# Attention and feed-forward in one kernel: the last batch's attention listed ahead of batch 14's gates, without idle matmuls

## The chip, the cores and the metric

One of the cores of a Trainium2 chip runs the kernel. The metric is the device time of one execution in microseconds (us). Of the kernel before, three timed runs and one profiled execution are shown. In the profile, PE is TensorE (PEld its weight loads), DVE is VectorE, ACT is ScalarE, POOL is GpSimd and SP is SyncE, which issues the transfers.

## The reference, cut to what matters

The input is x of 16 batches x 1024 rows x 256 columns in float32. `_layernorm` divides by sqrt(var + 1e-5) and has no weights.

```python
x = x + _layernorm(attn(_layernorm(x)))     # Q, K, V of width 256; softmax(Q K^T / 16) V
x = x + _layernorm(ffn(_layernorm(x)))      # h = silu(gate) * up, 768 wide; h @ w_down^T
```

Gate, up and down weights are integers times 1/127. Both residual additions take the unnormalised x.

## The kernel before

**Numbers and matmuls.** Every float32 operand of a large matmul is split into a high and a low half in float16 (`...h`, `...l`), and a product is made of two or three float16 passes, all recorded at line 868 (`passes`). One full line of work therefore is: an engine computes a float32 tile, ScalarE writes the high half (`o_high`, `y_high`, `p_high`, `h_high`), VectorE or GpSimd the low one (`o_low`, `y_low`, `p_low`, `h_low`), and where rows have to become columns SyncE turns both halves by a DMA transpose (`turn_x`, `turn_p`, `turn_y`).

**The work of one batch b.** The 1024 rows are 8 tiles of 128, in two groups g of four tiles. `project_z(b, g)` multiplies x by a product of the Q and K weights. `score(b, i)` makes the 128 x 1024 scores of tile i, 12 matmuls of 512 columns; `row_max`, `exp`, `p_high`, `p_low` and `turn_p` follow. `attend(b, g, u)` (line 1014) multiplies the turned probabilities by x, 12 matmuls of 512 columns; u // 2 is the half dh of the columns, u % 2 the first or second half of the keys. So four calls finish a group, and `o_high` (520) and `o_low` (751) of each dh follow its second call. `project_v(b, g)` (1028) applies the V weights, 24 matmuls of 256 columns, and leaves V of four tiles in the PSUM banks 4 and 5.

**From V to y.** VectorE scales V by the softmax sums (`y_scale`, 762, two tiles a call) and takes its statistics (`y_stats`, 771). GpSimd makes the inverse deviation (`y_norm`, 389: lines 327 and 331, then 334 and 336). VectorE adds to x and takes the statistics of the sum (`x1_add`, 783: line 790 twice, then 795 and 799; it reads the banks 4 and 5, half 0 bank 4, half 1 bank 5). GpSimd normalises again (`x1_norm`, 401). ScalarE writes y (`y_hat`, 526) and its high half (`y_high`, 534), GpSimd the low half (`y_low`, 409), SyncE turns both. Only then can `gate_up(b, g, c)` run (1042): 4 matmuls of 512 columns for the gate, 4 for up, in two neighbouring banks, for one of six chunks c of h.

**From gates to the result.** ScalarE applies `silu` (540), VectorE multiplies (`h_mul`, 801), then `h_high` (548) and `h_low` (415; VectorE makes it for c = 2 and 5, GpSimd for the others). The buffer `hf` has three places, so `silu` of chunk n waits for `h_low` of chunk n - 3. `down(b, g, pair)` (1051) multiplies by the down weights, 24 matmuls of 256 columns, into bank 4 (pair 0) or 5 (pair 1), the same banks as V. `d_stats`, `d_norm`, `d_add` and `add_bias` normalise and add, and `store` writes the result. The last group's down projection is `last_down`, followed by the functions `last_...`.

**What sets the order.** Every engine has a list of calls written out by hand, and runs it strictly in that order. An engine waits on semaphores inside a call; what is behind that call in its list waits too. A loop `for b in range(1, 13)` (PE; ScalarE's runs over 2 to 13) holds the steady state, in which batch b + 1's scores run among batch b's attention and gates. Behind the loop, batches 13 to 15 are listed call by call: from line 1184 for SyncE, 1341 for GpSimd, 1578 for ScalarE, 1886 for VectorE, 2107 for TensorE. The pair `(name, n)` in a TensorE call is what its bank waits for:

```python
            down(t, 14, 0, 0, (x1_done, 118), three)
            gate_up(t, 14, 1, 5, 2, (silu_done, 178), (hmul_done, 178), three)
            keep_busy(t, 36, ol_done[1], 32, 7)
            gate_up(t, 15, 0, 0, 6, (ol_done[0], 32), (ol_done[1], 32), three)
```

`(x1_done, 4n + k)` with n = 2b + g means that k tiles of group (b, g) have been added; `(ft_done[pair], 2n + 2)` that `d_add` has read the bank of that pair; `(silu_done, k)` and `(hmul_done, k)` that chunk k - 1, counted over all batches, has been read out of its bank. `keep_busy(t, n, sem, value, bank)` (892) issues n matmuls of 256 columns on a constant, whose result nobody reads; line 897 records them. There is one call of 36 of them, at line 2171, and two at the start of the program. `reload(s, b, g)` (260) loads x again for the residual sum into one of four buffers; its wait on `stored` is for the stores that last used that buffer. The calls of batch 14 and 15 that the text speaks of stand at the lines 2145 to 2188 (TensorE), 1716 to 1724 (the end of ScalarE's list), 1993 to 2005 (`x1_add` of batch 15), 1214 and 1240 (`reload`).

In the profiled run the flag is 0, so `three` is False: `gate_up` has 8 matmuls and `down` 24.

## Time and profile before

| what | before |
|---|---|
| median of three runs (lowest to highest) | 1363.91 us (1363.36 to 1363.94) |
| the profiled execution | 1363.66 us, of which the span of the profile 1361.90 us |
| TensorE busy | 1347.7 us, 99% of the span |
| VectorE, ScalarE, GpSimd busy | 901.8, 878.1, 832.4 us (66%, 64%, 61%) |
| granted clock of TensorE, mean | 1.00 |
| idle matmuls of line 897 | 66: 30 at the start, 36 behind line 2170 |
| HBM traffic | 39 GB/s over the span |

The span runs from the first to the last instruction of the trace. A row of a timeline gives the start and the duration in us, the engine, the line, the operation, its output and its inputs; xN means N such operations merged, and square brackets the idle time before them and what ended it. TensorE's matmuls overlap: each shows 0.38 us for 512 columns and 0.27 us for 256, but the next one starts before it ends, so the distance of two starts is what one costs.

### The profile page before, as it was taken

How to read it: one execution, taken by the hardware profiler on the slowest of the kernel's cores; microseconds unless marked ns; L12 is line 12 of the kernel's file. 1: busy time of each engine (PE TensorE's matmuls, PEld its weight loads, DVE VectorE, ACT ScalarE, POOL GpSimd, SP SyncE). 2: the span in 40 equal slices, each digit the busy share in tenths (PEclk: the TensorE clock that was granted, in tenths of full speed). 3: DMA queues.
4: the chain of work that ended last, by engine and by line, in shares of the span. 5: the costliest groups of instructions: out<-in, count | busy, mean ns of one | idle time of the engine just before them, and what ended most of it. 6: DMA issues, size and time to landing. Idle time of an engine off the chain costs nothing.

```text
span 1361.9 us, 22402 instructions
## 1 busy us (share of the span) xinstructions
PE 1347.7 (99%) x7414; PEld 725.8 (53%) x7414; DVE 901.8 (66%) x2167; ACT 878.1 (64%) x1378; POOL 832.4 (61%) x1001
## 2 busy tenths in 40 slices
PE   8999999999999999999999999999999999999998
PEld 5445455555555555555554555545555555555555
DVE  7895675666766666666766657667666676656556
ACT  6765775666757577475665766567566675756645
POOL 5686483765847648475584746748376584754635
PEclk9999999999999999999999999999999999999999
DMA  5996482835638366392753827448373563725512
GB/s 180 184 194 138 88 153 79 140 101 115 133 86 157 68 132 140 70 169 65 131 132 71 162 79 127 121 92 147 80 142 100 114 134 86 136 66 100 110 32 64
DMA packets 432968, 157.24 MB, mean 115 GB/s; under 512 B 413905, under 2 KB 416337, under 8 KB 432850
## 3 DMA queue, kind: packets, MB, share of 16 engines
q1 hardware_dynamic: 432048, 154.99, 55.2%
q8 instruction: 61, 1.00, 0.3%
q10 hardware_dynamic: 802, 0.79, 0.2%
q14 instruction: 57, 0.47, 0.1%
HBM read 36.70 MB, written 16.78 MB: 39 GB/s over the span
## 4 chain that ended last, share of the span: by engine, by line
PE 92%; POOL 2%; DVE 2%; DMA 2%; ACT 1%; issue 1%; SPq 0%; DVEq 0%; ACTq 0%; POOLq 0%
PE S L868 91%; DMA yTl<-yl 1%; POOL xl L368 1%; POOL Pl L386 0%; POOL yl L413 0%; DVE st L721 0%; DVE S L768 0%; DMA xs<-in_L_attn_t 0%; DVE mxs L739 0%; POOL xs L356 0%; PE S L897 0%; DVE st L777 0%; ACT yn L531 0%; DMA xTl<-xl 0%; POOL rs L331 0%
## 5 line engine op out<-in xcount | busy, mean ns | idle before, releaser
L511 ACT ACTIVATE P<-S,nmx,sc 128x1024 f32<-128x1024 f32 x128 | 153.6, 1200 | 267.1 <-DVE nmx L743 264.9
L805 DVE SCALAR_TENSOR_TENSOR hf<-S,sc,hf 128x512 f32<-128x512 f32 x192 | 141.9, 746 | 140.8 <-ACT hf L546 135.2
L739 DVE TENSOR_REDUCE mxs<-S 128x1 f32<-128x1024 f32 x128 | 156.1, 1220 | 115.7 <-PE S L868 115.7
L386 POOL TENSOR_TENSOR Pl<-P,Ph 128x1024 f16<-128x1024 f32 x96 | 205.1, 2138 | 30.1 <-issue 26.0
L868 PE MATMUL S<-PTh,xh 128*128 128x512 f16 x512 | 194.1, 379 | 0.0
L868 PE MATMUL S<-PTl,xh 128*128 128x512 f16 x512 | 194.0, 379 | 0.0
L868 PE MATMUL S<-PTh,xl 128*128 128x512 f16 x512 | 194.0, 379 | 0.0
L868 PE MATMUL S<-xTh,zTh 128*128 128x512 f16 x506 | 191.8, 379 | 2.0 <-ACT P L511 1.0
L868 PE MATMUL S<-xTh,zTl 128*128 128x512 f16 x508 | 192.5, 379 | 0.0
L868 PE MATMUL S<-xTl,zTh 128*128 128x512 f16 x508 | 192.5, 379 | 0.0
L327 POOL TENSOR_SCALAR rs<-mv,sc 128x2 f32<-128x2 f32 (+2 forms) x96 | 34.6, 361 | 227.4 <-DVE mv L781 184.9
L422 POOL TENSOR_TENSOR hTl<-hf,hTh 128x512 f16<-128x512 f32 x128 | 146.4, 1158 | 42.4 <-ACT hTh L553 42.4
L868 PE MATMUL S<-Wh,hTh 128*128 128x256 f16 x768 | 170.3, 273 | 0.0
L868 PE MATMUL S<-Wh,hTl 128*128 128x256 f16 x768 | 170.3, 273 | 0.0
L546 ACT ACTIVATE hf<-S,sc 128x512 f32<-128x512 f32 x192 | 130.6, 682 | 52.5 <-POOL hTl L422 37.7
L331 POOL TENSOR_TENSOR rs<-rs,mhalf 128x4 f32<-128x4 f32 (+2 forms) x160 | 145.5, 909 | 13.3
L868 PE MATMUL S<-yTh,Gh 128*128 128x512 f16 x384 | 145.6, 379 | 2.4 <-DMA yTl<-yl 2.4
L868 PE MATMUL S<-yTl,Gh 128*128 128x512 f16 x384 | 145.5, 379 | 0.0
L868 PE MATMUL S<-yTh,Uh 128*128 128x512 f16 x384 | 145.5, 379 | 0.0
L868 PE MATMUL S<-yTl,Uh 128*128 128x512 f16 x384 | 145.5, 379 | 0.0
L553 ACT ACTIVATE hTh<-hf 128x512 f16<-128x512 f32 x192 | 119.5, 624 | 35.4 <-DVE hf L805 35.4
L518 ACT ACTIVATE Ph<-P 128x1024 f16<-128x1024 f32 x128 | 134.8, 1054 | 4.2 <-DMA PTl<-Pl 1.1
(155 smaller groups left out, 2486.0 us busy)
## 6 DMA issues: line engine op xcount, KB each, us to landing
xs<-in_L_attn_t SPq DMA_DIRECT2D x32, 512.0 KB, 5.3
...
out_x<-X SPq DMA_DIRECT2D x62, 256.0 KB, 2.9
PTh<-Ph SPq DMA_TRANSPOSE x128, 3.2
PTl<-Pl SPq DMA_TRANSPOSE x128, 3.2
...
```

The costliest lines, as they stand in the source:

```text
L327: p.engine.tensor_scalar(rs, var, scalar1=eps, scalar2=mul, op0=ALU.add, **({} if mul is None else {"op1": ALU.mult})).then_inc(g_step, 1)
L331: return p.engine.tensor_tensor(out=rs, in0=rs, in1=mhalf[:, 0:rs.shape[1]], op=ALU.pow)
L368: p.engine.tensor_tensor(out=xl[k][:, gs, :], in0=src, in1=xh[k][:, gs, :], op=ALU.subtract).then_inc(xl_done if b else xl0_done, 1)
L386: p.engine.tensor_tensor(out=Pl[:, m % 3, :], in0=P[:, m % 2, :], in1=Ph[:, m % 3, :], op=ALU.subtract).then_inc(pl_vector if i in PL_ON_V ...
L422: p.engine.tensor_tensor(out=hTl[g][:, c, :], in0=hf[:, n % 3, :], in1=hTh[g][:, c, :], op=ALU.subtract).then_inc(hl_vector if c in HL_ON_ ...
L511: a.engine.activation(P[:, m % 2, :], ps[:, bank:bank + 2, :].rearrange("p a n -> p (a n)"), ACT.Exp, bias=nmx[:, c:c + 1], scale=sS, accu ...
L518: a.engine.activation(Ph[:, m % 3, :], P[:, m % 2, :], ACT.Copy).then_inc(ph_done, 1)
L546: a.engine.activation(hf[:, n % 3, :], ps[:, bank, :], ACT.Silu, scale=sc2[:, 3:4]).then_inc(silu_done, 1)
L553: a.engine.activation(hTh[g][:, c, :], hf[:, n % 3, :], ACT.Copy).then_inc(hh_done, 1)
L739: v.engine.tensor_reduce(mxs[:, c:c + 1], ps[:, bank:bank + 2, :].rearrange("p a n -> p (a n)"), axis=AX.X, op=ALU.max, negate=True).then_ ...
L805: v.engine.scalar_tensor_tensor(out=hf[:, n % 3, :], in0=ps[:, bank + 1, :], scalar=sc2[:, 4:5], in1=hf[:, n % 3, :], op0=ALU.mult, op1=AL ...
L868: done = t.engine.matmul(out, s, m, start=(start and i == 0), stop=(stop and i == len(terms) - 1))
```

## The change

The lists of all five engines behind the loop are written anew; no function changes. In TensorE's list `attend(15, 0, 3)` and `project_v(15, 0)` go ahead, all of batch 15's attention and both of its V projections stand in front of the last three gates of batch 14, `down(14, 0, 0)` and `down(14, 0, 1)` go behind those, and the 36 idle matmuls are gone. The pairs that the four `down` calls and the `project_v` calls wait for follow the new order of use of the banks 4 and 5. In the other lists calls change places; the number of calls of each kind is the same. `last_bias` moves from the end of ScalarE's list to the middle of batch 15's gates. The diff, cut to its core:

```diff
--- before.py
+++ after.py
@@ -1183,68 +1183,68 @@
+            store(s, 12, 0, 0)
             turn_p(s, 14, 0, 0)
             turn_p(s, 14, 0, 1)
-            store(s, 12, 0, 0)
             store(s, 12, 0, 1)
+            reload(s, 14, 0)
             turn_p(s, 14, 1, 0)
+            turn_p(s, 14, 2, 0)
             turn_p(s, 14, 1, 1)
-            turn_p(s, 14, 2, 0)
             turn_p(s, 14, 2, 1)
             turn_p(s, 14, 3, 0)
...
+            turn_x(s, 15, 0, 0)
             turn_y(s, 13, 0, 1)
-            turn_x(s, 15, 0, 0)
             turn_x(s, 15, 0, 1)
+            turn_x(s, 15, 1, 0)
             turn_p(s, 14, 5, 0)
+            turn_x(s, 15, 1, 1)
             turn_p(s, 14, 5, 1)
             turn_p(s, 14, 6, 0)
             turn_p(s, 14, 6, 1)
-            turn_x(s, 15, 1, 0)
-            turn_x(s, 15, 1, 1)
             turn_p(s, 14, 7, 0)
-            turn_p(s, 14, 7, 1)
             turn_y(s, 13, 1, 0)
             turn_y(s, 13, 1, 1)
             store(s, 12, 1, 0)
             store(s, 12, 1, 1)
-            reload(s, 14, 0)
+            turn_p(s, 14, 7, 1)
...
+            reload(s, 15, 0)
             turn_p(s, 15, 5, 1)
             turn_p(s, 15, 6, 0)
             turn_p(s, 15, 6, 1)
-            store(s, 13, 0, 1)
             turn_y(s, 14, 1, 0)
             turn_y(s, 14, 1, 1)
             turn_p(s, 15, 7, 0)
+            store(s, 13, 1, 1)
             turn_p(s, 15, 7, 1)
-            store(s, 13, 1, 1)
-            reload(s, 15, 0)
             reload(s, 15, 1)
-            store(s, 14, 0, 0)
-            store(s, 14, 0, 1)
             turn_y(s, 15, 0, 0)
             turn_y(s, 15, 0, 1)
             turn_y(s, 15, 1, 0)
             turn_y(s, 15, 1, 1)
+            store(s, 14, 0, 0)
+            store(s, 14, 0, 1)
...
@@ -1338,26 +1338,26 @@
             x_low(p, 15, 0)
             p_low(p, 14, 5)
+            x_low(p, 15, 1)
+            p_low(p, 14, 6)
             y_norm(p, 13, 1)
-            p_low(p, 14, 6)
-            x_low(p, 15, 1)
-            p_low(p, 14, 7)
+            h_low(p, 13, 0, 0)
             x1_norm(p, 13, 1)
-            h_low(p, 13, 0, 0)
+            z_low(p, 15, 0)
             d_norm(p, 12, 1, 0)
             y_low(p, 13, 1)
             h_low(p, 13, 0, 1)
-            z_low(p, 15, 0)
+            h_low(p, 13, 0, 3)
             d_norm(p, 12, 1, 1)
-            h_low(p, 13, 0, 3)
             h_low(p, 13, 0, 4)
+            p_low(p, 14, 7)
...
@@ -1366,34 +1366,34 @@
+            p_low(p, 15, 7)
             h_low(p, 14, 0, 4)
-            p_low(p, 15, 7)
             h_low(p, 14, 1, 0)
-            d_norm(p, 14, 0, 0)
+            y_norm(p, 15, 0)
             h_low(p, 14, 1, 1)
-            d_norm(p, 14, 0, 1)
-            y_norm(p, 15, 0)
-            h_low(p, 14, 1, 3)
             x1_norm(p, 15, 0)
             y_low(p, 15, 0)
             y_norm(p, 15, 1)
+            h_low(p, 14, 1, 3)
             h_low(p, 14, 1, 4)
             x1_norm(p, 15, 1)
+            d_norm(p, 14, 0, 0)
+            d_norm(p, 14, 0, 1)
             y_low(p, 15, 1)
...
@@ -1575,133 +1575,134 @@
+            exp(a, 14, 2, 0)
             p_high(a, 14, 1)
-            exp(a, 14, 2, 0)
             p_high(a, 14, 2)
             exp(a, 14, 3, 2)
+            o_high(a, 13, 1, 1)
             p_high(a, 14, 3)
-            o_high(a, 13, 1, 1)
             exp(a, 14, 4, 0)
             p_high(a, 14, 4)
...
+            o_high(a, 15, 0, 1)
             silu(a, 14, 0, 5, 2)
+            silu(a, 14, 1, 0, 0)
             h_high(a, 14, 0, 5)
-            silu(a, 14, 1, 0, 0)
-            add_bias(a, 13, 1, 1)
+            h_high(a, 14, 1, 0)
             silu(a, 14, 1, 1, 2)
-            h_high(a, 14, 1, 0)
             h_high(a, 14, 1, 1)
+            o_high(a, 15, 1, 0)
+            y_hat(a, 15, 0, 0)
+            o_high(a, 15, 1, 1)
             silu(a, 14, 1, 2, 0)
-            h_high(a, 14, 1, 2)
-            o_high(a, 15, 0, 1)
-            add_bias(a, 14, 0, 0)
-            silu(a, 14, 1, 3, 2)
-            add_bias(a, 14, 0, 1)
-            h_high(a, 14, 1, 3)
-            o_high(a, 15, 1, 0)
-            o_high(a, 15, 1, 1)
-            silu(a, 14, 1, 4, 0)
-            y_hat(a, 15, 0, 0)
             y_hat(a, 15, 0, 1)
             y_high(a, 15, 0)
+            h_high(a, 14, 1, 2)
+            silu(a, 14, 1, 3, 2)
+            silu(a, 14, 1, 4, 0)
+            h_high(a, 14, 1, 3)
             h_high(a, 14, 1, 4)
             silu(a, 14, 1, 5, 2)
+            y_hat(a, 15, 1, 0)
+            silu(a, 15, 0, 0, 6)
+            y_hat(a, 15, 1, 1)
+            silu(a, 15, 0, 1, 0)
             h_high(a, 14, 1, 5)
-            silu(a, 15, 0, 0, 6)
-            y_hat(a, 15, 1, 0)
-            y_hat(a, 15, 1, 1)
             y_high(a, 15, 1)
-            silu(a, 15, 0, 1, 0)
+            silu(a, 15, 0, 2, 2)
             h_high(a, 15, 0, 0)
-            silu(a, 15, 0, 2, 2)
             h_high(a, 15, 0, 1)
             h_high(a, 15, 0, 2)
+            add_bias(a, 14, 0, 0)
+            add_bias(a, 14, 0, 1)
             silu(a, 15, 0, 3, 6)
+            last_bias(a)
             silu(a, 15, 0, 4, 0)
+            silu(a, 15, 0, 5, 2)
             h_high(a, 15, 0, 3)
-            silu(a, 15, 0, 5, 2)
             h_high(a, 15, 0, 4)
...
@@ -1720,7 +1721,6 @@
             add_bias(a, 15, 0, 1)
-            last_bias(a)
             last_centre(a)
@@ -1902,131 +1902,131 @@
...
             z_float(v, 15, 0, 0)
             h_mul(v, 13, 0, 1, 2)
             d_stats(v, 12, 1, 0)
             h_mul(v, 13, 0, 2, 6)
+            d_add(v, 12, 1, 0)
             d_stats(v, 12, 1, 1)
-            h_low(v, 13, 0, 2)
             h_mul(v, 13, 0, 3, 0)
             h_mul(v, 13, 0, 4, 2)
-            d_add(v, 12, 1, 0)
             z_float(v, 15, 1, 6)
+            d_add(v, 12, 1, 1)
+            h_low(v, 13, 0, 2)
             h_mul(v, 13, 0, 5, 0)
-            d_add(v, 12, 1, 1)
             h_mul(v, 13, 1, 0, 2)
+            h_mul(v, 13, 1, 1, 6)
             h_low(v, 13, 0, 5)
-            h_mul(v, 13, 1, 1, 6)
...
             h_mul(v, 14, 0, 0, 6)
+            h_mul(v, 14, 0, 1, 0)
             x1_add(v, 14, 1, 0)
-            h_mul(v, 14, 0, 1, 0)
             h_mul(v, 14, 0, 2, 2)
+            h_mul(v, 14, 0, 3, 6)
             x1_add(v, 14, 1, 1)
-            h_mul(v, 14, 0, 3, 6)
-            h_low(v, 14, 0, 2)
             row_max(v, 15, 7, 2)
             h_mul(v, 14, 0, 4, 0)
+            h_low(v, 14, 0, 2)
             d_stats(v, 13, 1, 1)
             row_inverse(v, 15, 1)
             d_add(v, 13, 1, 1)
+            o_low(v, 15, 0, 0)
+            o_low(v, 15, 0, 1)
             h_mul(v, 14, 0, 5, 2)
-            o_low(v, 15, 0, 0)
+            h_mul(v, 14, 1, 0, 0)
             h_low(v, 14, 0, 5)
-            h_mul(v, 14, 1, 0, 0)
+            y_scale(v, 15, 0, 0)
+            y_stats(v, 15, 0, 0)
+            y_scale(v, 15, 0, 1)
+            y_stats(v, 15, 0, 1)
             h_mul(v, 14, 1, 1, 2)
-            d_stats(v, 14, 0, 0)
-            d_stats(v, 14, 0, 1)
-            h_mul(v, 14, 1, 2, 0)
-            d_add(v, 14, 0, 0)
-            h_low(v, 14, 1, 2)
-            d_add(v, 14, 0, 1)
-            o_low(v, 15, 0, 1)
-            y_scale(v, 15, 0, 0)
-            y_scale(v, 15, 0, 1)
-            y_stats(v, 15, 0, 0)
-            y_stats(v, 15, 0, 1)
-            h_mul(v, 14, 1, 3, 2)
             x1_add(v, 15, 0, 0)
             x1_add(v, 15, 0, 1)
             o_low(v, 15, 1, 0)
             o_low(v, 15, 1, 1)
+            h_mul(v, 14, 1, 2, 0)
+            y_scale(v, 15, 1, 0)
+            y_stats(v, 15, 1, 0)
+            y_scale(v, 15, 1, 1)
+            y_stats(v, 15, 1, 1)
+            h_mul(v, 14, 1, 3, 2)
             h_mul(v, 14, 1, 4, 0)
-            y_scale(v, 15, 1, 0)
-            y_scale(v, 15, 1, 1)
-            y_stats(v, 15, 1, 0)
-            y_stats(v, 15, 1, 1)
+            x1_add(v, 15, 1, 0)
+            x1_add(v, 15, 1, 1)
+            h_low(v, 14, 1, 2)
+            d_stats(v, 14, 0, 0)
             h_mul(v, 14, 1, 5, 2)
-            x1_add(v, 15, 1, 0)
+            d_stats(v, 14, 0, 1)
+            d_add(v, 14, 0, 0)
+            h_mul(v, 15, 0, 0, 6)
+            d_add(v, 14, 0, 1)
+            h_mul(v, 15, 0, 1, 0)
             h_low(v, 14, 1, 5)
-            x1_add(v, 15, 1, 1)
-            h_mul(v, 15, 0, 0, 6)
-            h_mul(v, 15, 0, 1, 0)
             h_mul(v, 15, 0, 2, 2)
             d_stats(v, 14, 1, 0)
...
@@ -2152,31 +2152,30 @@
             down(t, 13, 1, 1, (x1_done, 120), three)
             attend(t, 15, 0, 0, (silu_done, 172))
             attend(t, 15, 0, 1)
+            attend(t, 15, 0, 3)
             gate_up(t, 14, 0, 5, 2, (exp_done, 128), (exp_done, 128), three)
             gate_up(t, 14, 1, 0, 0, (silu_done, 173), (hmul_done, 173), three)
+            project_v(t, 15, 0, (ft_done[0], 56), (ft_done[1], 56))
+            attend(t, 15, 1, 0, (ol_done[0], 31))
             gate_up(t, 14, 1, 1, 2, (silu_done, 174), (hmul_done, 174), three)
-            down(t, 14, 0, 0, (x1_done, 118), three)
-            down(t, 14, 0, 1, (ft_done[1], 56), three)
-            gate_up(t, 14, 1, 2, 0, (silu_done, 175), (hmul_done, 175), three)
-            attend(t, 15, 0, 3)
-            attend(t, 15, 1, 0, (ol_done[0], 31))
-            project_v(t, 15, 0, (ft_done[0], 58), (ft_done[1], 58))
-            gate_up(t, 14, 1, 3, 2, (silu_done, 176), (hmul_done, 176), three)
             attend(t, 15, 1, 1)
             attend(t, 15, 1, 2, (ol_done[1], 31))
             attend(t, 15, 1, 3)
+            gate_up(t, 14, 1, 2, 0, (silu_done, 175), (hmul_done, 175), three)
+            project_v(t, 15, 1, (x1_done, 122), (x1_done, 124))
+            gate_up(t, 14, 1, 3, 2, (silu_done, 176), (hmul_done, 176), three)
             gate_up(t, 14, 1, 4, 0, (silu_done, 177), (hmul_done, 177), three)
-            project_v(t, 15, 1, (x1_done, 122), (x1_done, 124))
             gate_up(t, 14, 1, 5, 2, (silu_done, 178), (hmul_done, 178), three)
-            keep_busy(t, 36, ol_done[1], 32, 7)
+            down(t, 14, 0, 0, (x1_done, 126), three)
+            down(t, 14, 0, 1, (x1_done, 128), three)
             gate_up(t, 15, 0, 0, 6, (ol_done[0], 32), (ol_done[1], 32), three)
             gate_up(t, 15, 0, 1, 0, (silu_done, 179), (hmul_done, 179), three)
             gate_up(t, 15, 0, 2, 2, (silu_done, 180), (hmul_done, 180), three)
-            down(t, 14, 1, 0, (x1_done, 126), three)
+            down(t, 14, 1, 0, (ft_done[0], 58), three)
             gate_up(t, 15, 0, 3, 6, (silu_done, 181), (hmul_done, 181), three)
             gate_up(t, 15, 0, 4, 0, (silu_done, 182), (hmul_done, 182), three)
             gate_up(t, 15, 0, 5, 2, (silu_done, 183), (hmul_done, 183), three)
-            down(t, 14, 1, 1, (x1_done, 128), three)
+            down(t, 14, 1, 1, (ft_done[1], 58), three)
             gate_up(t, 15, 1, 0, 6, (silu_done, 184), (hmul_done, 184), three)
             gate_up(t, 15, 1, 1, 0, (silu_done, 185), (hmul_done, 185), three)
             down(t, 15, 0, 0, (ft_done[0], 60), three)
```

## Rows read from the trace of the kernel before

**Rows 1.** The page: busy time, the chain that ended last, DMA issues

```profile
PE 1347.7 (99%) x7414; PEld 725.8 (53%) x7414; DVE 901.8 (66%) x2167; ACT 878.1 (64%) x1378; POOL 832.4 (61%) x1001
...
PE 92%; POOL 2%; DVE 2%; DMA 2%; ACT 1%; issue 1%; SPq 0%; DVEq 0%; ACTq 0%; POOLq 0%
...
out_x<-X SPq DMA_DIRECT2D x62, 256.0 KB, 2.9
```

**Rows 2.** Waits of TensorE from 40 us on: total us, times, longest us

```profile
PE S L868 <- DMA yTl<-yl: 2.4, 4, 1.4
PE S L868 <- ACT P L511: 1.0, 1, 1.0
```

**Rows 3.** Stretches: length, busy time of PE, PEld, DVE, ACT, POOL, granted clock, DMA

```profile
101.00:104.00 3.00, 2.56 (x12) 1.18 (x13) 0.76 (x2) 2.97 (x5) 1.13 (x3) 1.00 1.03 197
1300.00:1320.00 20.00, 20.00 (x123) 11.77 (x122) 14.67 (x45) 8.74 (x15) 9.10 (x15) 1.00 0.18 41
...
1360.00:1362.00 2.00, 0.00 (x0) 0.00 (x0) 0.00 (x0) 0.00 (x0) 0.00 (x0) 0.74 0.33 122
```

**Rows 4.** Timeline of TensorE

```profile
1195.80 0.38 PE L868 MATMUL S<-yTh,Gh 128*128 128x512 f16 x1
...
1266.39 0.39 PE L868 MATMUL S<-xTh,zTh 128*128 128x512 f16 x1
...
1313.54 0.27 PE L868 MATMUL S<-Vh,oTl 128*128 128x256 f16 x1
1313.65 0.38 PE L868 MATMUL S<-yTh,Gh 128*128 128x512 f16 x1
...
1315.38 0.82 PE L897 MATMUL S<-ident 128*128 128x256 f16 x6
...
1319.42 0.39 PE L868 MATMUL S<-yTh,Gh 128*128 128x512 f16 x1
```

**Rows 5.** Timeline of SyncE's DMA queue

```profile
1144.17 1.06 SPq L288 DMA_DIRECT2D out_x<-X  x2
...
1191.87 1.23 SPq L282 DMA_TRANSPOSE yTl<-yl  x1
...
1316.30 1.23 SPq L282 DMA_TRANSPOSE yTl<-yl  x1
```

**Rows 6.** Transfers into yTl between 1300 and 1340 us

```profile
DMA to landing us min/median/max: 3.1/3.1/3.1
```

**Rows 7.** Timeline of VectorE

```profile
1264.94 1.39 DVE L805 SCALAR_TENSOR_TENSOR hf<-S,sc,hf 128x512 f32<-128x512 f32 x2
...
1299.96 1.67 DVE L768 SCALAR_TENSOR_TENSOR S<-S,rinv,bvb 128x256 f32<-128x256 f32 x4 [3.89 <-PE S L868]
...
1313.85 1.67 DVE L768 SCALAR_TENSOR_TENSOR S<-S,rinv,bvb 128x256 f32<-128x256 f32 x4 [1.92 <-PE S L868]
...
1318.83 0.88 DVE L790 SCALAR_TENSOR_TENSOR X<-S,rs,X 128x256 f32<-128x256 f32 x2 [0.92 <-POOL rs L331]
...
1321.09 0.87 DVE L790 SCALAR_TENSOR_TENSOR X<-S,rs,X 128x256 f32<-128x256 f32 x2
...
1356.08 0.43 DVE L837 BATCH_NORM_STATS2 st<-S 128x6 f32<-128x256 f32 x1 [0.46 <-PE S L868]
...
1357.16 1.66 DVE L861 SCALAR_TENSOR_TENSOR X<-zw,rs,X 128x256 f32<-128x256 f32 x4
```

**Rows 8.** Timeline of GpSimd

```profile
1310.10 0.23 POOL L336 TENSOR_SCALAR nb<-nb 128x4 f32<-128x4 f32 x1
...
1317.76 1.04 POOL L331 TENSOR_TENSOR rs<-rs,mhalf 128x4 f32<-128x4 f32 x1
```

**Rows 9.** Timeline of ScalarE

```profile
1309.46 0.60 ACT L524 ACTIVATE oTh<-S 128x512 f16<-128x512 f32 x1 [4.29 <-PE S L868]
...
1310.91 2.06 ACT L531 ACTIVATE yn<-X,nb,rs 128x256 f32<-128x256 f32 x4
...
1354.35 1.69 ACT L571 ACTIVATE X<-X,c 128x256 f32<-128x256 f32 x4
```

More of the change, by code:

```diff
@@ L1226, in _ @@
             turn_y(s, 14, 0, 0)
+            turn_p(s, 15, 4, 0)
             turn_y(s, 14, 0, 1)
-            turn_p(s, 15, 4, 0)
+            store(s, 13, 0, 1)
             turn_p(s, 15, 4, 1)
             turn_p(s, 15, 5, 0)
+            reload(s, 15, 0)
             turn_p(s, 15, 5, 1)
@@ L1340, in _ @@
                 x_norm(p, b + 3, 1)
+            p_low(p, 14, 2)
             y_norm(p, 13, 0)
-            p_low(p, 14, 2)
+            p_low(p, 14, 3)
             x1_norm(p, 13, 0)
-            p_low(p, 14, 3)
             y_low(p, 13, 0)
@@ L1368, in _ @@
             p_low(p, 15, 0)
+            p_low(p, 15, 2)
             y_norm(p, 14, 0)
-            p_low(p, 15, 2)
             x1_norm(p, 14, 0)
@@ L1404, in _ @@
             h_low(p, 15, 1, 0)
+            h_low(p, 15, 1, 1)
             d_norm(p, 15, 0, 0)
-            h_low(p, 15, 1, 1)
             h_low(p, 15, 1, 3)
@@ L1587, in _ @@
             y_hat(a, 13, 0, 1)
+            o_high(a, 13, 1, 0)
             y_high(a, 13, 0)
-            o_high(a, 13, 1, 0)
             x_high(a, 15, 0)
+            x_high(a, 15, 1)
             exp(a, 14, 5, 2)
             p_high(a, 14, 5)
-            x_high(a, 15, 1)
             exp(a, 14, 6, 0)
@@ L1621, in _ @@
             silu(a, 13, 1, 3, 2)
-            add_bias(a, 12, 1, 1)
             h_high(a, 13, 1, 2)
@@ L1628, in _ @@
             h_high(a, 13, 1, 5)
+            add_bias(a, 13, 0, 0)
             o_high(a, 14, 0, 1)
             o_high(a, 14, 0, 0)
-            add_bias(a, 13, 0, 0)
+            add_bias(a, 13, 1, 0)
             exp(a, 15, 0, 0)
+            exp(a, 15, 1, 2)
             p_high(a, 15, 0)
-            exp(a, 15, 1, 2)
             p_high(a, 15, 1)
@@ L1637, in _ @@
             p_high(a, 15, 2)
-            add_bias(a, 13, 1, 0)
             exp(a, 15, 3, 2)
+            o_high(a, 14, 1, 0)
             p_high(a, 15, 3)
-            o_high(a, 14, 1, 0)
             y_hat(a, 14, 0, 0)
+            y_hat(a, 14, 0, 1)
             exp(a, 15, 4, 0)
-            p_high(a, 15, 4)
-            y_hat(a, 14, 0, 1)
             y_high(a, 14, 0)
             o_high(a, 14, 1, 1)
+            p_high(a, 15, 4)
+            add_bias(a, 13, 0, 1)
             exp(a, 15, 5, 2)
@@ L1932, in _ @@
             h_mul(v, 13, 1, 5, 0)
+            h_low(v, 13, 1, 5)
             d_stats(v, 13, 0, 0)
-            h_low(v, 13, 1, 5)
             d_add(v, 13, 0, 0)
+            o_low(v, 14, 0, 1)
             d_stats(v, 13, 1, 0)
-            o_low(v, 14, 0, 1)
+            d_add(v, 13, 1, 0)
             o_low(v, 14, 0, 0)
@@ L2011, in _ @@
             h_mul(v, 15, 0, 3, 6)
+            d_add(v, 14, 1, 0)
             h_mul(v, 15, 0, 4, 0)
-            d_add(v, 14, 1, 0)
             h_mul(v, 15, 0, 5, 2)
+            h_low(v, 15, 0, 5)
             d_stats(v, 14, 1, 1)
-            h_low(v, 15, 0, 5)
+            h_mul(v, 15, 1, 0, 6)
             d_add(v, 14, 1, 1)
-            h_mul(v, 15, 1, 0, 6)
             h_mul(v, 15, 1, 1, 0)
```

68 lines of the change are left out of this document (34 added, 34 removed).

## The prediction

> **What bounds the kernel.** I read the page first: TensorE is busy 99% of the span and carries 92% of the chain that ended last, while VectorE, ScalarE and GpSimd are at 61 to 66% [rows 1]. So a change counts only where TensorE waits, where it does work that need not be done, and in what follows its last matmul. The waits of TensorE come next: from 40 us on it stands still for 3.4 us in all, its longest waits being 1.4 and 1.0 us [rows 2], and the same view from 1130 us on, where the edits lie, has no line for it. In the table of stretches the 20 us from 1300 hold 20.00 us of TensorE work at a granted clock of 1.00 [rows 3]. Dense, but not all useful: 36 of those matmuls are `keep_busy` (line 2171), from 1315.38 to the first matmul of `gate_up(15,0,0)` at 1319.42 [rows 4]. That is 4.04 us, in which the kernel in truth waits for batch 15's first y: its low half is issued for turning at 1316.30 and lands 3.1 us later, at 1319.4 [rows 5, 6]. The matmul starts at that moment, so the fillers just cover the wait.
>
> **Units.** The eight matmuls of 512 columns of one `gate_up` take 1.73 us (1313.65 to 1315.38), so two start 0.216 us apart; two of 256 columns start 0.11 us apart [rows 4], 0.109 over a long run. So `attend` and `score` (12 of 512) take 2.59 us, `gate_up` (8 of 512) 1.73 us, `project_v` and `down` (24 of 256) 2.62 us. The diff leaves the number of real matmuls as it is; only their order changes.
>
> **TensorE's order.** I put the calls end to end with these units. Both kernels run `attend(15,0,1)` up to about 1279.8 (in the time of before). Then, after: `attend(15,0,3)`, two gates, `project_v(15,0)` from 1285.9 to 1288.5, where before it is 1297.1 to 1299.8: batch 15's attention is 11.3 us ahead. Between the end of `project_v(15,0)` and `gate_up(15,0,0)` before has 15.6 us of work and the fillers; after has four attends, five gates, one `project_v` and two downs: 2.59 x 4 + 1.73 x 5 + 2.62 x 3 = 26.9 us. The chain from V to y took 19.4 us (1299.96, the first scaling, to 1319.4) [rows 5 to 7], so it is covered with some 7 us to spare, and **the 4.04 us go**.
>
> **What the new order puts in the way.** `down(14,0,0)` writes the bank from which `x1_add(15,1,0)` still reads V, and now waits for `(x1_done, 126)`. Before, with 1313.65 as the next call's first matmul after `project_v(15,1)`, the scaling starts at 1313.85 and the pair of adds runs 1318.83 to 1319.71 [rows 4, 7]: 6.06 us. Inside lie 3.4 us of scaling and statistics and the inverse deviation on GpSimd, which ends at 1318.80 [rows 8]. In the new list `h_mul(14,1,3)` and `h_mul(14,1,4)`, 0.73 us each, fall into GpSimd's 1.5 us and cost nothing; scaling and statistics are only interleaved. TensorE starts 0.06 us after such a product (1264.94 + 1.39 = 1266.33, to 1266.39) [rows 4, 7], so at 6.12. Up to there it has three gates, 5.19 us. **A new wait of 0.93 us.** Behind it in TensorE's queue stand both downs and all of batch 15's gates, so all of it counts. `down(14,0,1)` wants the second pair of adds, 2.3 us later than the first by their rows [rows 7], less some 0.6 for the `h_low` between them that is now behind: 1.7, under the 2.62 us of the first down. Bounds of the wait: 0.4 us if the adds come half a microsecond sooner, 1.6 if an `h_mul` misses its gap (0.73).
>
> The second half of `gate_up(14,1,5)` wants `h_mul(14,1,3)`, ready some 0.2 us too late; that shifts nothing, as `down` waits longer anyway. Further on, `silu(14,1,5)` waits behind the adds and `h_low(14,1,2)`; its product is ready about 11.5 us after `project_v(15,1)`, `gate_up(15,0,2)` wants it at 14.8. `down(14,1,0)` wants `h_low(14,1,5)` in its second half at 17.2; I work it out at 16.2.
>
> **The feed of the moved calls.** `project_v(15,0)` needs `o_high(15,0,1)` and `o_low(15,0,1)` after `attend(15,0,3)`: 0.6 us [rows 9] and 0.7 (like an `h_mul` on the same engine, half of 1.39 [rows 7]) under two gates, 3.45 us. `project_v(15,1)` has one gate (1.73 us) over the same pair, as before; but ScalarE now has `y_hat(15,0,0)` ahead of `o_high(15,1,1)`. Its input came 10.4 us after the scaling began (1299.96 to 1310.33) [rows 7, 8], so at 1299.1 where the scaling starts at 1288.7; two of its tiles take 1.04 [rows 9], to 1300.2; `attend(15,1,3)` ends at 1300.75. Spare: 0.55 us, cost nothing. If the cover goes, each further microsecond costs one.
>
> **Batches 13 and 14 in the new lists.** TensorE's order is unchanged there and dense. One wait vanishes: the second half of `score(15,7)` was due at 1266.32 and stood 0.07 us for `h_mul(14,0,2)` [rows 4, 7]; that product ends 0.7 us earlier once `h_mul(14,0,1)` is listed ahead of `x1_add(14,1,0)`. The narrowest places: turning y of (13,1) was issued at 1191.87, `gate_up(13,1,0)` begins at 1195.80 [rows 4, 5]; with 3.1 us to land, 0.8 us are spare. GpSimd now has `z_low(15,0)` (2.7 us) ahead of `y_low(13,1)` and `p_low(14,7)` (2.1 us) behind it; going through its list I get the issue 0.2 us later, up to 0.6. And `h_low(13,0,2)` now stands behind `d_add(12,1,1)`, so `silu(13,0,5)` comes some 2 us later, at about 1198.2, and its product by 1199.4; the second half of `gate_up(13,1,2)`, 4.3 us after 1195.80, wants it at 1200.1. Cost nothing, bound 0.5 us each.
>
> **SP's queue.** `reload(14,0)` now waits for the landing of both stores of (12,0) with `turn_p(14,1,0)` to the last behind it: issued until about 1145.2 [rows 5], landing 2.9 us later [rows 1], plus up to 2 us of issue, till 1150. `turn_p(14,1,0)` gets its input only at about 1151.1, as `exp(14,2)` now goes first; no loss. `reload(15,0)` holds `turn_p(15,5,1)`, for which `attend(15,1,0)` asks some 28 us later. The stores of (14,0) go behind the turnings of (15,y), since their downs are now late; ahead of them they would have closed the queue.
>
> **The end.** `last_bias` leaves ScalarE's end: 1.69 us from 1354.35 [rows 9], which the chain of waits counts as critical. But VectorE takes the statistics of the last tile at 1356.08, as soon as TensorE is done, and its four last adds follow without a gap, 1.66 us from 1357.16 [rows 7]. So 0, bound 0.1 us of gain. At its new place it holds `silu(15,0,4)` until about 1328.0; its bank is wanted at 1333.6.
>
> **Sum:** -4.04 + 0.93 - 0.07 = **-3.2 us**. The profiled execution took 1363.66 us for a span of 1361.90; it stands 0.25 below the median of the runs, 1363.91. So some 1360.7 as median. About 0.2% (2.7 us, a limit at 1361.2) is what a measurement of this kernel tells from no change; the forecast is 0.5 us past it.
>
> **The clock.** The granted clock stayed at 1.00 through the wait of 1.4 us at 101 us [rows 2, 3]; it fell (0.74 over the last 2 us) only when TensorE had done nothing since about 1356 [rows 3, 7]. So the new wait costs its own length. The Trainium skill, "TensorE: Matmul & The Clock Gate" (section "Part 1: The HAM clock gate"), says that half rate is the default and recent activity lifts it; by that rule idle products are worth their time where a wait would be long, which speaks against taking them out. Here the rows leave the sum at -3.2.
>
> **Rivals.**
> (A) The forecast, one new wait of 0.4 to 1.6 us: 1360.2 to 1361.4. Chance 0.57.
> (B) No new wait, as the adds come early enough: -4.1, 1359.8. Against it: the adds' 6.06 us hold a fixed order of work on two engines. 0.08.
> (C) A second wait upstream, 1 to 2.5 us: ScalarE's `y_hat(15,0,0)` holds `o_high(15,1,1)` and so `project_v(15,1)`, or y of (13,1) or `silu(13,0,5)` comes late. For it: spares of 0.5 to 0.9 us, worked out from many rows, in a schedule never seen. 1361.7 to 1363.3, say 1362.4. 0.23.
> (D) Nothing gained: the edited lists of VectorE, ScalarE and GpSimd lose in batches 13 and 14 what the fillers give, 3 to 4 us. 1363.9. 0.07.
> (E) Slower: at the wait before `down(14,0,0)` the clock falls to the lower of its two levels. Price: a gate is 1.73 us dearer, a down 2.62. It decides from 3.2 us of such loss, two downs (5.2 us), which gives 1365.9. Against it: the clock rows above. 0.05.
> By the Trainium skill's rule, were it to bite, the time is that of (E).
>
> **Numbers.** Faster: A nearly whole (0.52), B (0.08), a little of C (0.05): 0.65. Same: the rest of A, most of C, D: 0.29. Slower: 0.06. The range begins just under (B), at 1359.7, and takes in most of C, to 1362.9; above it stay D, E and the end of C, some 0.15, below it next to nothing.
>
> **What would show it.** Right: no L897 row after 100 us; TensorE's waits list DVE X L790, once, 0.4 to 1.6 us, near 1310; turning of (15,0) issued near 1304.5 and 1306.6; last adds near 1354; clock 1.00. Wrong: waits on ACT oTh or DVE oTl (C), on DMA yTl or DVE hf between 1130 and 1280 (C, D), a clock below 1.00 after 1310 (E), or no wait at all (B).

## The result, and the profile after

The changed kernel takes **1361.71 us** (median of 22 runs, 1361.10 to 1362.43) against 1364.19 for the kernel before (22 runs, 1363.09 to 1364.78) on the same chip. The ratio is 0.9983, 95% interval 0.9977 to 0.9989: 2.48 us less, a little under the 0.2% (2.7 us) that the prediction took as the line to no change, though the interval leaves out 1. The forecast was 3.2 us less. Its profiled execution took 1361.76 us for a span of 1359.9. A few executions of the later runs took 200 to 3000 us longer at a lower granted clock, and every measured time given for a kernel is the median of the others.

The page, against [rows 1]: TensorE is 3.1 us less busy, with 36 matmuls fewer, and still carries by far the largest share of the chain that ended last, now 88% where it was 92%.

```profile
PE 1344.6 (99%) x7378; PEld 722.2 (53%) x7378; DVE 903.6 (66%) x2167; ACT 877.1 (65%) x1378; POOL 831.5 (61%) x1001
...
PE 88%; DVE 3%; POOL 2%; DMA 2%; SPq 2%; issue 1%; ACT 1%; DVEq 0%; ACTq 0%; POOLq 0%
```

Waits of TensorE from 40 us on (total us, times, longest), against [rows 2]: the last line is new, and it is the only wait behind 1130 us.

```profile
PE S L868 <- DMA yTl<-yl: 2.5, 4, 1.6
PE S L868 <- ACT P L511: 1.0, 1, 1.0
PE S L868 <- DVE X L790: 0.9, 1, 0.9
```

Timeline of TensorE, against [rows 4]: the first matmul of `down(14,0,0)` with its wait, and the last matmul of all. The one ahead of the wait starts at 1310.24 and the next was due at 1310.46, so it costs 1.01 us.

```profile
1311.47 0.27 PE L868 MATMUL S<-Wh,hTh 128*128 128x256 f16 x1 [0.85 <-DVE X L790]
...
1353.03 0.27 PE L868 MATMUL S<-Wh,hTl 128*128 128x256 f16 x1
```

Timeline of VectorE, against [rows 7]: the pair of `h_mul` in the gap that GpSimd leaves, the pair of adds that TensorE waits for (it ends at 1311.32), and the last adds, 2.7 us earlier than before.

```profile
1308.79 1.39 DVE L805 SCALAR_TENSOR_TENSOR hf<-S,sc,hf 128x512 f32<-128x512 f32 x2
1310.44 0.88 DVE L790 SCALAR_TENSOR_TENSOR X<-S,rs,X 128x256 f32<-128x256 f32 x2 [0.26 <-POOL rs L331]
...
1354.43 1.67 DVE L861 SCALAR_TENSOR_TENSOR X<-zw,rs,X 128x256 f32<-128x256 f32 x4
```

SyncE's queue, against [rows 5]: the turnings of batch 15's first y, `store(15,0,1)`, and the two last stores, of which the second waits for the last add.

```profile
1304.71 1.24 SPq L282 DMA_TRANSPOSE yTh<-yh  x1
1306.92 1.23 SPq L282 DMA_TRANSPOSE yTl<-yl  x1
...
1350.34 0.33 SPq L288 DMA_DIRECT2D out_x<-X  x1
1355.72 1.98 SPq L295 DMA_DIRECT2D out_x<-X  x2
```

The two last stores of the kernel before:

```profile
1358.45 1.05 SPq L295 DMA_DIRECT2D out_x<-X  x2
```

**Where the rest went.** Behind the last add the span runs on for 1359.9 - 1356.10 = 3.8 us; before it was 1361.9 - 1358.82 = 3.1. So 0.7 us were lost behind the last computation, and the last matmul and the last add kept their distance (3.05 and 3.07 us). The spans of these two traces lie only 2.0 us apart, since in the trace of the changed kernel what is ahead of `project_v(14,1)`, where TensorE's order is unchanged, took 0.40 us longer (it starts at 1255.89 us against 1255.49); over all 14 traces that start lies between 1254.65 and 1256.74. Two views of the transfers show where, each from 1.3 us ahead of the end of the last add: GB/s in 40 slices of a stretch of 4.5 us, what the queue q8 moved (the view calls it an instruction queue), and issue to landing. First before:

```profile
GB/s 0 0 0 0 146 0 0 0 0 0 0 0 0 0 0 137 300 382 382 410 437 355 437 410 301 264 355 346 146 0 0 0 0 0 0 0 0 0 0 0
...
q8 instruction: 1, 0.02, 1.6%
...
out_x<-X SPq DMA_DIRECT2D x1, 128.0 KB, 2.5
```

Then after:

```profile
GB/s 0 0 0 0 0 0 0 0 0 0 0 0 146 0 0 191 328 355 300 410 382 382 410 410 137 0 27 27 27 27 173 309 373 264 82 18 27 0 0 0
...
q8 instruction: 1, 0.02, 1.5%
...
out_x<-X SPq DMA_DIRECT2D x1, 128.0 KB, 3.3
```

The lone 146 is a transfer of 16 KB on q8, from here on the fetch. In most of the run one comes for some 128 matmuls (after: 129, 125 and 129 start between those at 1215.6, 1238.3, 1260.2 and 1285.4 us), so it is probably TensorE that is fed. The last ones come closer: between the three at 1348.2, 1353.2 and 1356.2 lie 44 matmuls and none, and no run shows what sets them. The fetch keeps one of the 16 DMA engines for 1.15 us (1.6% of 16 x 4.5). Before, it starts 0.84 us ahead of the end of the last add and is over at +0.31; the stores' data begin at about +0.4 and flow in one piece. After, it starts 0.12 us behind that end and is over at +1.20, so it overlaps the stores' data. Right behind it, from +1.5 on, the stores fall to 27 GB/s for half a microsecond. That is one packet of 3 KB in each slice, about a fifteenth of the full rate, as if only the engine that had the fetch were still at work on its share. SyncE's issue of the last store takes 1.58 us, where before it took 0.66, and the data flow again 0.45 us after it ends. Both last stores land in 3.3 us, where before they took 2.7 and 2.5.

The Trainium skill's page "DMA: Bandwidth & Descriptors" (section "Queues, rings and completion order") says that a DMA engine takes its queues in turn and changes only at the end of a packet. The rows fit that, but do not prove it: the view counts the fetch as one packet, and the store's share of one engine comes late behind it. Which engine it is they do not show.

### The profile page after: what moved, and what is told of

It reads as the page before. It is cut to its first block, busy times and chain, and to the rows that moved or that the text cites. A ratio compares the mean times of both kernels' runs of the same rounds, so it can differ in the third digit from the quotient of the medians.

```text
span 1359.9 us, 22330 instructions
## 1 busy us (share of the span) xinstructions
PE 1344.6 (99%) x7378; PEld 722.2 (53%) x7378; DVE 903.6 (66%) x2167; ACT 877.1 (65%) x1378; POOL 831.5 (61%) x1001
## 4 chain that ended last, share of the span: by engine, by line
PE 88%; DVE 3%; POOL 2%; DMA 2%; SPq 2%; issue 1%; ACT 1%; DVEq 0%; ACTq 0%; POOLq 0%
PE S L868 88%; DMA yTl<-yl 1%; SPq L276 1%; DVE S L768 1%; POOL xl L368 1%; DVE st L777 1%; POOL Pl L386 1%; DVE mxs L739 0%; POOL yl L413 0%; SPq L257 0%; DVE st L721 0%; ACT Ph L518 0%; POOL rs L331 0%; POOL xs L356 0%; DMA xs<-in_L_attn_t 0%
```

## The experiments

Two measures are used beside the time. **TensorE's part** is the time from a call whose order is the same in both kernels to the last matmul: from the first matmul of `project_v(14,1)`, 100.28 us before and 97.14 after; from that of `project_v(15,0)`, 66.87 after (the other traces with after's order agree to 0.01 from that second call on). **Early** and **late** tell where `d_add(15,0,1)` stands on VectorE: ahead of `h_mul(15,1,5)`, as in after, or behind `h_low(15,1,5)`, as before. **The tail** is from the end of the last add to the end of the span. Ratios are to the kernel before, run on the same chip.

### The changed kernel again

Edit: none.

> The changed kernel unaltered, for a second trace on the chip that the next kernels share. Three accounts of why the measured gain is 2.5 us where the sum gave 3.2. Theory 1 (the last stores): the two last transfers to out_x are always issued and landed later when store (15, 0, 1) has gone out some 5 us ahead of them; then the span again ends 3.7 to 3.9 us after the end of the last addition, against 3.1 in the trace of before, and the gain is 2.4 to 2.6 us. Rival 2 (chance): the issue of these stores varies from execution to execution by some 0.7 us; then this trace may as well show 3.1 us. Rival 3 (drift): before and after differed by up to 0.4 us in stretches where their code is the same, against the changed kernel; then a second trace may have the loop's end 0.3 to 0.4 us earlier. The wait of TensorE for the addition of y to x at the head of down (14, 0, 0) stands again, 0.8 to 1.1 us, in every account.

Measured: 1361.77 us, ratio 0.9984 (0.9975 to 0.9993). TensorE's part is 97.14 again, the wait at `down(14,0,0)` too, the tail 3.9 us. The 0.7 us behind the last add are lost again, which speaks against chance, and against drift as an account of the tail. The start of `project_v(14,1)` did move, to 1255.30 us, so drift there is real, and the measured 2.07 us under before is a little less than the first 2.48.

### What of the end does it

`end_back` is the changed kernel with this edit, `end_back2` the same once more, and `end_alone` is the kernel before with the reverse edit.

```diff
-            d_add(v, 15, 0, 1)
             h_mul(v, 15, 1, 5, 2)
             h_low(v, 15, 1, 5)
+            d_add(v, 15, 0, 1)
```

> The changed kernel with one thing put back: d_add (15, 0, 1) behind h_mul and h_low (15, 1, 5) on VectorE, as before the change, so that store (15, 0, 1) is issued some 4 us later, right ahead of the last stores. Theory 1 (the last stores lose 0.7 us where that store has gone out early): the span ends 3.0 to 3.2 us after the last addition and the kernel takes 0.5 to 0.7 us less than the changed one. Rival 2 (chance): equal to the changed kernel within 0.2 us in the median. Nothing of TensorE waits for h_mul (15, 1, 5) in the trace of the changed kernel, so TensorE's stretch stays the same in either account.

Measured: 1360.86 us, ratio 0.9978 (0.9968 to 0.9987), 0.91 us under the changed kernel on the same chip. TensorE's part stays at 97.14, the tail is 3.5 us. Theory 1 had the direction right and the size of the tail (3.0 to 3.2) too small; of the 0.9 us the traces show only 0.4 in the tail (3.9 to 3.5).

> The kernel before with one part of the change alone: d_add (15, 0, 1) ahead of h_mul (15, 1, 5) on VectorE. TensorE's work is untouched. Theory 1: the span ends 3.7 to 3.9 us after the last addition instead of 3.1, and the kernel takes 0.5 to 0.7 us more than before. Rival 2: the same as before within 0.2 us. If h_mul (15, 1, 5) were late for down (15, 1, 0) by the 0.6 us of the addition, TensorE would show a wait of up to 0.6 us there; the trace of the changed kernel shows none.

Measured: 1364.81 us, ratio 1.0009 (1.0000 to 1.0018), 0.97 us over before. TensorE's part 100.27, the tail 4.0 us. Both ways round, the early place of one call of 0.87 us on VectorE, which hides in idle time, costs 0.9 to 1.0 us of the whole.

`store_late` is the changed kernel with

```diff
+            s.wait_ge(last_st, 3)
             store(s, 15, 0, 1)
```

> The changed kernel with store (15, 0, 1) held back on SP until the statistics of the last tiles are there (near 1352.5 us instead of 1350.3), and nothing moved on VectorE. It parts the two things that end_back did together. Seen so far: with that store 5.4 us ahead of the first last store the span ended 3.8 to 4.0 us after the last addition (three traces), with 4.0 us between them 3.1 to 3.5 us (three traces). Theory 1 (the distance of the stores decides): with 3 us between them the span ends 3.0 to 3.4 us after the last addition and the time is 0.5 to 1.0 us below the changed kernel's. Rival (the order on VectorE decides, or it is chance): as the changed kernel within 0.2 us, 3.8 to 4.0 us after the last addition.

Measured: 1361.77 us, ratio 0.9978 (0.9969 to 0.9987), tail 3.7 us. The store is now 3.0 us ahead of the last ones, nearer than the 4.0 of before, and yet the tail is longer than before's 3.1. So in this trace the distance of the stores, theory 1 as put there, does not set the tail. The time speaks less plainly: the ratio is that of `end_back`, and 2.74 us under before on its chip is 0.3 to 0.7 more than the changed kernel (measured twice) and `after_shift` reached, while the profiled execution, 1362.49 us, is one of the slowest of its eleven. So one trace speaks against theory 1, and the time leaves it open. What orders the tails is when the 16 KB fetch is over; the table below has them all.

### The fillers

`no_fill` is the kernel before with

```diff
-            keep_busy(t, 36, ol_done[1], 32, 7)
```

> The kernel before without its 36 matmuls that compute nothing (the keep_busy call ahead of gate_up (15, 0, 0)); nothing else is changed. TensorE then waits for o_low (15, 1, 1) and the yTl of batch 15 instead of filling the time. Theory (these matmuls only cover a wait, the order sets the time): a wait of 3.9 to 4.1 us stands in their place, the granted clock stays at 1.00 behind it, and the time is that of before within 0.3 us. Rival (clock): a stretch of 4 us without matmuls brings TensorE to the lower clock for the gates of batch 15 behind it; at 2.6 us for half a gate set, several us more, so over 1 us slower than before. Rival (the matmuls held something up): faster by 0.1 us or more.

Measured: 1365.88 us, ratio 1.0016 (1.0008 to 1.0025): 2.0 us **slower**. The theory fell on the clock and the time, its wait of 3.9 us is there, and the rival with the clock holds. TensorE's part is 102.83, 2.55 us more than before. Stretches of this kernel (columns as in [rows 3]):

```profile
1315.00:1316.00 1.00, 0.00 (x0) 0.00 (x0) 1.00 (x6) 0.00 (x0) 0.43 (x1) 1.00 0.78 145
1316.00:1317.00 1.00, 0.00 (x0) 0.00 (x0) 1.00 (x4) 0.00 (x0) 0.39 (x2) 0.98 0.36 73
1317.00:1318.00 1.00, 0.00 (x0) 0.00 (x0) 0.08 (x2) 0.63 (x1) 0.95 (x1) 0.50 1.01 189
...
1322.00:1323.00 1.00, 1.00 (x4) 0.43 (x3) 0.75 (x1) 0.00 (x0) 0.83 (x2) 0.50 0.00 0
1323.00:1324.00 1.00, 1.00 (x5) 0.34 (x3) 0.00 (x0) 0.00 (x0) 0.82 (x3) 0.61 0.00 0
```

And its timeline of TensorE:

```profile
1318.59 0.61 PE L868 MATMUL S<-yTh,Gh 128*128 128x512 f16 x1 [3.89 <-DMA yTl<-yl]
1318.99 0.63 PE L868 MATMUL S<-yTl,Gh 128*128 128x512 f16 x1
...
1323.69 0.43 PE L868 MATMUL S<-yTh,Uh 128*128 128x512 f16 x1
1323.95 0.38 PE L868 MATMUL S<-yTl,Uh 128*128 128x512 f16 x1
```

TensorE has nothing to do from 1314.7 on; near 1317 the granted clock goes to 0.50, the level of 1.2 GHz, and stays there until 1323.7. Twelve matmuls in a row take 5.10 us (1318.59 to 1323.69) where 12 x 0.216 = 2.6 would do: the 2.5 us lost. It was back at 1.00 behind them. So the idle products of before did not only cover a wait, they kept the clock. The Trainium skill's rule, given in the prediction from "TensorE: Matmul & The Clock Gate" (section "Part 1: The HAM clock gate"), is borne out here. The changed kernel can do without them because its order has no such wait: its own is 1.0 us, through which the clock stays at 1.00.

`fill_back` is the changed kernel with

```diff
+            keep_busy(t, 36, ol_done[1], 32, 7)
             gate_up(t, 15, 0, 0, 6, (ol_done[0], 32), (ol_done[1], 32), three)
```

> The changed kernel with the 36 matmuls that compute nothing put back in front of gate_up (15, 0, 0). Theory (in the new order nothing is left there to wait for, so they are pure time): TensorE's work ends 3.9 to 4.1 us later than in the changed kernel and the time is 3.8 to 4.2 us above it, near 1365.7 us. Rival (the changed order only moved the wait, and part of the 4 us would be spent waiting in any case): less than 3 us above it, and other waits of TensorE behind the call go.

Measured: 1366.30 us, ratio 1.0013 (1.0004 to 1.0022), 0.0030 above the changed kernel's 0.9983, or 4.1 us. From `project_v(15,0)` to the last matmul it is 70.80 us against 66.87, 3.93 more. In the new order nothing is waited for there.

### The new wait

`gate_only` is the changed kernel with

```diff
+            gate_up(t, 15, 0, 0, 6, (ol_done[0], 32), (ol_done[1], 32), three)
             down(t, 14, 0, 0, (x1_done, 126), three)
             down(t, 14, 0, 1, (x1_done, 128), three)
-            gate_up(t, 15, 0, 0, 6, (ol_done[0], 32), (ol_done[1], 32), three)
```

> The changed kernel with gate_up (15, 0, 0) ahead of down (14, 0, 0) on TensorE, nothing else moved. The wait of 1.0 us for the addition goes, since the gate covers 1.73 us of it and its own inputs landed at 1310.0, 0.4 us before it is due. Worked out from the trace of the changed kernel, the time comes back as a wait at down (14, 1, 0) or at a gate of batch 15, as h_low (14, 1, 5) and h_high (14, 1, 5) are queued behind silu and h_mul of batch 15: theory A: a new wait of 0.7 to 1.0 us there, within 0.3 us of the changed kernel. Rival B (those steps move up with TensorE): 0.9 to 1.1 us less than the changed kernel, no wait of TensorE over 0.2 us behind 1303 us.

Measured: 1364.47 us, ratio 0.9999 (0.9990 to 1.0008), where the changed kernel has 0.9983; from `project_v(15,0)` to the last matmul it is 68.91 us, 2.04 more. Neither theory has that. TensorE's waits behind 1303 us:

```profile
PE S L868 <- DVE hTl L422: 1.8, 1, 1.8
PE S L868 <- DMA yTl<-yl: 0.9, 1, 0.9
```

The first was foreseen in kind and was mis-sized by a factor of two. The second was not foreseen. The granted clock stayed at 1.00 through both.

`gate_first` is `gate_only` with both calls moved up, on ScalarE and on VectorE:

```diff
             y_hat(a, 15, 1, 0)
+            h_high(a, 14, 1, 5)
...
-            h_high(a, 14, 1, 5)
...
             d_stats(v, 14, 0, 1)
+            h_low(v, 14, 1, 5)
...
-            h_low(v, 14, 1, 5)
```

> The kernel gate_only with h_high (14, 1, 5) right behind y_hat (15, 1, 0) on ScalarE and h_low (14, 1, 5) right behind d_stats (14, 0, 1) on VectorE, so that what down (14, 1, 0) needs is done sooner. Theory: no wait of TensorE is left behind 1303 us and the kernel takes 0.9 to 1.1 us less than the changed one, near 1360.8 us. Rival: the added work ahead of silu (15, 0, 0) and h_mul (15, 0, 0) makes the gates of batch 15 late, and 0.3 us or less is gained.

Measured: 1362.03 us, ratio 0.9983 (0.9974 to 0.9992), no gain over the changed kernel. The wait for `hTl` is gone and that for `yTl` stays: from `project_v(15,0)` to the last matmul 66.96. The turning into `yTl` was issued in time, at 1307.07, but landed after 4.6 us. GB/s in 40 slices from 1308 to 1312 us:

```profile
GB/s 0 0 210 174 215 212 197 202 166 54 18 0 0 0 0 0 3 8 8 10 10 8 10 10 10 102 276 297 287 277 22 0 0 0 0 0 0 0 0 0
...
q8 instruction: 1, 0.02, 2.2%
...
yTl<-yl SPq DMA_TRANSPOSE x1, 4.6
```

The fetch began at 1308.25. The turning stops near 1309.1, trickles at 10 GB/s, and catches up from 1310.4 on. In `gate_only` the fetch began at 1309.50 and the landing took 4.5 us.

`gf_shift` is `gate_first`, and `after_shift` the changed kernel, with this edit of `keep_busy`, whose calls at the start are left:

```diff
-            for _ in range(n):
-                t.engine.matmul(ps[:, bank, 0:256], words[:, 0:128], words[:, :], start=True, stop=True)
+            for _ in range(2 * n):
+                t.engine.matmul(ps[:, bank, 0:128], words[:, 0:128], words[:, 0:128], start=True, stop=True)
```

> The kernel gate_first with each matmul of 256 columns in the two calls of keep_busy at the start (24 and 6 of them, behind 3 us and 12 us) replaced by two of 128 columns: the same columns, and 30 more matmuls with their weight loads in TensorE's stream of instructions, 1300 us ahead of the place in question. In gate_first and gate_only a 16 KB transfer of the queue that fetches instructions (q8, one for every 128 or so matmuls) started at 1308.25 and 1309.50, among the packets of the transpose into yTl, whose landing took 4.6 and 4.5 us instead of 3.1, and TensorE waited 0.9 us for it. Theory (this collision ate the gain): the fetch now falls some 4 to 5 us earlier, ahead of both transposes or on the first of them, yTl lands in 3.1 to 3.3 us, the wait of 0.9 us goes or shrinks under 0.3, and the kernel takes 0.6 to 1.0 us less than gate_first, if the fetch at the end stays where it is. Rival (the landing is long for another reason, as the order of TensorE's work): 4.5 us again and no difference from gate_first beyond 0.2 us.

Measured: 1360.37 us, ratio 0.9975 (0.9965 to 0.9985), against 0.9983 for `gate_first`; the two intervals overlap, so here the traces carry the argument. The fetch is at 1302.72, `yTl` lands in 3.1 us, TensorE has no wait behind 1303, and its part from `project_v(15,0)` is 65.87: 1.09 less than `gate_first`, 1.00 less than after. The same turning, GB/s from 1307 to 1311 us:

```profile
GB/s 0 0 0 97 220 215 223 220 207 220 205 197 220 192 190 165 51 0 0 0 0 0 0 0 0 0 0 0 0 0 0 0 0 0 0 0 0 0 0 0
...
yTl<-yl SPq DMA_TRANSPOSE x1, 3.1
```

> The changed kernel with the same replacement at the start alone, the control for gf_shift. Theory: its fetch near 1312.6 also moves 4 to 5 us earlier and may lengthen a transpose into yTh or yTl, but gate_up (15, 0, 0) is due at 1316.7 there, over 5 us after the landing, so the time stays within 0.3 us of the changed kernel (1361.7 to 1361.9 us). Rival (the replacement changes the start or the loop): a difference of over 0.3 us, seen in the trace by the start of the first projection of V at 67.3 us or the last one at 1302.6 us.

Measured: 1361.78 us, ratio 0.9982 (0.9973 to 0.9991), the changed kernel's time. The fetch near 1312.6 went to 1303.76 and `down(14,0,0)` waits as before it (66.88). The rows are not untouched elsewhere, so the equal time is a balance and not stillness: a wait of 1.6 us for `yTl` near 101 us went, with others of 0.7 and 0.3 in its place; between `project_v(14,1)` and `project_v(15,0)` it takes 30.63 us against after's 30.25, with a new wait of 0.2 for `yTl`; and the tail is 4.6.

> The kernel end_back unaltered, a second time, for a firmer number and a second trace of its end. Theory: the last q8 fetch again starts before the last addition ends, the span ends 3.4 to 3.6 us after that addition, and the time is 0.5 to 1.1 us below the changed kernel's, ratio to before 0.9976 to 0.9980. Rival (the first measurement was luck): within 0.3 us of the changed kernel.

Measured: 1361.03 us, ratio 0.9976 (0.9967 to 0.9985), 0.75 under `after_shift` on the same chip; tail 3.4 us. The first measurement holds.

> gf_shift with d_add (15, 0, 1) put back behind h_low (15, 1, 5) as in end_back: the version that should be the fastest. In ten traces so far the span ended 3.1 us after the last addition where the last q8 fetch started 0.85 us ahead of that addition's end, 3.5 us (three traces) where it started 0.02 to 0.49 us ahead, and 3.8 to 4.5 us (six traces) where it started 0.1 to 0.8 us behind it, among the packets of the last stores. Theory: both collisions avoided, 1.0 us of wait at the head of batch 15 and 0.4 to 0.9 us at the end: 1.4 to 1.9 us under the changed kernel, near 1360.0 us against 1363.9 for before. Rival (the collision at yTl stays, only the end gains): as end_back, 0.5 to 1.0 us under the changed kernel.

Measured: **1359.55 us, ratio 0.9970 (0.9960 to 0.9981)**, 4.6 us under before and 2.2 under `after_shift` beside it. TensorE's part from `project_v(15,0)` 65.86, tail 3.1. It beats both kernels. It differs from `gf_shift` in the place of `d_add(15,0,1)` alone: the tail is 3.1 us instead of 4.3, the median 0.82 us lower. The gain is more than the two terms foreseen against the changed kernel: in the traces 2.9 us lie between `after_shift` and this one, of which the tail has 1.5, TensorE's part from `project_v(14,1)` 1.06 (97.51 to 96.45), and the rest what lies ahead.

### The tail and the fetch, all 14 traces

Start of the last 16 KB fetch of queue q8, counted from the end of the last add, how long it took, when it was over, and the tail:

| kernel | `d_add(15,0,1)` | fetch starts, us | takes | over at | tail, us |
|---|---|---|---|---|---|
| before | late | -0.84 | 1.1 | +0.3 | 3.1 |
| best_shift | late | -0.83 | 1.1 | +0.3 | 3.1 |
| end_back2 | late | -0.39 | 1.1 | +0.8 | 3.4 |
| no_fill | late | -0.49 | 1.3 | +0.8 | 3.5 |
| end_back | late | -0.01 | 0.9 | +0.9 | 3.5 |
| store_late | early | -0.31 | 1.4 | +1.1 | 3.7 |
| after | early | +0.12 | 1.1 | +1.2 | 3.8 |
| after_again | early | +0.22 | 1.1 | +1.3 | 3.9 |
| end_alone | early | +0.19 | 1.3 | +1.5 | 4.0 |
| gf_shift | early | +0.15 | 1.6 | +1.7 | 4.3 |
| gate_first | early | +0.23 | 1.5 | +1.7 | 4.3 |
| fill_back | early | +0.84 | 0.9 | +1.8 | 4.4 |
| gate_only | early | +0.35 | 1.6 | +1.9 | 4.5 |
| after_shift | early | +0.35 | 1.7 | +2.1 | 4.6 |

The moment when the fetch is over puts all 14 tails in order, which its start alone does not (`store_late` against `end_back`). A fetch that is over when the stores' data begin, at +0.4, costs nothing; one that overlaps them costs 0.3 to 1.5 us. The fetch took 1.1 us in before and `best_shift`, where it met no other transfer, and up to 1.7 us where it met the stores. So the two seem to hold each other up, and its length is in part an effect and not only a cause. What the order of `d_add(15,0,1)` does shows in the fetch before the last: it starts 0.85 to 0.88 us ahead of the last matmul in the five traces with the call late, 0.13 to 0.32 us behind it in eight with the call early, and 0.35 ahead in `store_late`. The last one follows 3.1 to 3.9 us later.

**Left open.** Why VectorE's order moves the fetch by 1 us: `h_mul` and `h_low(15,1,5)` start at the same moments against the last matmul in after and `end_back` (4.93 and 3.41 us ahead). And that the collision causes the longer tail rests on these 14 traces and on the stall in the rows; the last fetch was not moved by itself. That the place of `d_add(15,0,1)` costs the time is shown, by a change in each direction; that it does so through the fetch is argued.

## Why the prediction was right, and where it was not

- **The fillers go, -4.04.** Right. Put back in the new order they cost 3.93 us (`fill_back`). What its own count left out is why they were there; only its paragraph on the clock points that way. Leaving them out of the old order costs 2.55 us of TensorE's time (`no_fill`). The step "the fillers just cover the wait" was half the truth; the sum did not need the other half.
- **The new wait, 0.93.** Right: 1.01, at the call and for the adds it named. The step was short by the start of TensorE behind the add, taken as 0.06 us and measured as 0.15 (1311.32 to 1311.47). The 0.2 us by which it saw the second half of `gate_up(14,1,5)` late are not in the trace (1309.37 to 1309.58, the usual distance); they were not in its sum.
- **-0.07 at `score(15,7)`.** Right, no such gap is left. The three terms with the wait as measured give -3.10; TensorE's part fell by 3.14.
- **The feed of the moved calls.** Right: `o_high(15,1,1)` had 0.60 us to spare, 0.55 worked out; turning issued at 1304.71 and 1306.92, 1304.5 and 1306.6 expected. Rival (C) did not come; no wait lies between 1130 and 1303.
- **The clock.** At 1.00 through the new wait; (E) was rightly put low for this kernel, and the mechanism is real: `no_fill` shows it with a wait of 3.9 us.
- **The end, priced at 0 with a bound of 0.1.** This is the step that failed. It looked at `last_bias` and stopped at the last add; it did not price `d_add(15,0,1)`, which the same edit moves ahead of `h_mul(15,1,5)`, and took what follows the last add as fixed. It cost 0.7 us in the trace, and 0.7 to 1.0 us in the medians of three comparisons (`end_back`, `end_alone`, `end_back2`). -3.14 and +0.7 make -2.4; measured -2.48.

So rival (A) came true for TensorE, and the time is 1.0 us above the 1360.7 that it gave: 0.7 us are the tail, which no rival had, and 0.28 come from the start of the sum, 1363.91 as the median of three runs of before where 22 runs have 1364.19. That takes it out of (A)'s own bounds, 1360.2 to 1361.4, and to the lower edge of (C)'s, whose wait did not come. The stated range holds it because room was left for (C), and that part is luck.
